# Quantising w1 and w3 to three values: a magnitude compare times half signs, with the signs formed on GpSimd

## The reference

```
xn = layernorm(x)
# recurrent branch (L = 256)
y      = gelu(xn @ w_y + b_y)
xb     = xn @ w_x + b_x
conv   = conv_b + sum_k conv_w[k] * xb shifted        # 4 taps over time
gate_x = sigmoid(conv @ w_ig + b_ig)
gate_a = sigmoid(conv @ w_ag + b_ag)
a      = exp(-8 * gate_a * softplus(a_param))
h[t]   = a[t] * h[t-1] + gate_x * conv * sqrt(1 - a^2)
attn   = (h * y) @ w_out + b_out
# feed-forward branch, hidden size 682, weights quantised on the device
s(w)   = mean(|w|)
q(w)   = clip(round(w / s), -1, 1) * s                # -s, 0 or +s
g      = silu(xn @ q(w1).T) * (xn @ q(w3).T)
ffn    = g @ q(w2).T
out    = x + attn + ffn
```

## Time and profile before

| | us |
|---|---|
| three runs | 77.08, 77.18, 77.36 |
| median | 77.18 |
| the profiled execution, its own time | 77.82 |
| its span in the profile | 76.0 |
| TensorE busy | 70.0 (92%) |
| VectorE busy | 60.8 (80%) |
| ScalarE busy | 49.9 (66%) |
| GpSimd busy | 33.4 (44%) |
| granted TensorE clock | 1.00 of full |

### The profile page before, as it was taken

How to read it: one execution, slowest core, us unless ns; L and a number is a source line. 1 busy time by engine, 2 the same in 40 slices (tenths; PEclk the granted TensorE clock), 3 DMA queues, 4 the chain that set the end, 5 groups by cost and what they waited for, 6 DMA issues and landing times.

```text
span 76.0 us, 1062 instructions
## 1 busy us (share of the span) xinstructions
PE 70.0 (92%) x364; PEld 60.1 (79%) x364; DVE 60.8 (80%) x99; ACT 49.9 (66%) x76; POOL 33.4 (44%) x43
## 2 busy tenths in 40 slices
PE   4999879999999799999999999499999999999960
PEld 4999768877887678888888889388888888899950
DVE  4887599999999999999989999169999999400340
ACT  3663714899999999999989768996357429100000
POOL 6385646336661750052007968940007818910000
DMA  0989999910000000000000000000000000340062
GB/s 13 259 212 338 349 405 367 361 67 9 0 0 0 4 0 0 0 0 0 5 1 0 0 9 0 0 0 0 0 0 0 0 0 0 111 165 9 0 207 69
DMA packets 5095, 5.63 MB, mean 74 GB/s; under 512 B 525, under 2 KB 4578, under 8 KB 5090
## 3 DMA queue, kind: packets, MB, share of 16 engines
q1 hardware_dynamic: 4946, 5.55, 21.8%
q10 hardware_dynamic: 144, 0.01, 0.1%
HBM read 4.51 MB, written 1.05 MB: 73 GB/s over the span
## 4 chain that ended last, share of the span: by engine, by line
PE 37%; ACT 33%; DVE 9%; DMA 7%; issue 5%; POOL 3%; SPq 3%; DVEq 0%; ACTq 0%
PE slot L670 12%; PE slot L703 11%; PE slot L714 9%; DMA x_sb<-x 7%; ACT ta L363 4%; POOL g_lo L256 3%; ACT tx L349 3%; ACT conv_hi L342 3%; ACT xn_y L324 3%; PE slot L653 2%; ACT ta L355 2%; SPq L186 2%; ACT g_hi L300 2%; DVE w_raw L515 2%; DVE stats L437 2%
## 5 line engine op out<-in xcount | busy, mean ns | idle before, releaser
L256 POOL TENSOR_TENSOR g_lo<-w_raw,g_hi 128x512 fp32r<-128x512 f32 x10 | 15.9, 1609 | 16.1 <-ACT g_hi L338 16.1
L670 PE MATMUL slot<-xt_lo,w_q 128*128 128x512 f32 x40 | 15.7, 394 | 0.0
L670 PE MATMUL slot<-xt_hi,w_q 128*128 128x512 f32 x40 | 15.7, 393 | 0.0
L703 PE MATMUL slot<-w_q,g_hi 128*128 128x256 f32 x40 | 10.2, 292 | 1.1 <-POOL g_lo L256 1.1
L703 PE MATMUL slot<-w_q,g_lo 128*128 128x256 f32 x40 | 9.8, 282 | 0.0
L332 ACT ACTIVATE w_raw<-slot,scale 128x512 f32<-128x512 f32 x10 | 6.8, 686 | 4.3 <-PE slot L670 4.3
L493 DVE SCALAR_TENSOR_TENSOR conv<-slot,par,conv 128x511 f32<-128x511 f32 (+2 forms) x12 | 9.0, 748 | 0.4
L703 PEld LDWEIGHTS slot<-w_q,g_hi 128*128 128x128 f32 x40 | 7.6, 191 | 1.6 <-POOL g_lo L256 1.6
L670 PEld LDWEIGHTS slot<-xt_lo,w_q 128*128 128x128 f32 x40 | 7.5, 188 | 1.7
L670 PEld LDWEIGHTS slot<-xt_hi,w_q 128*128 128x128 f32 x40 | 7.5, 188 | 1.7
L338 ACT ACTIVATE g_hi<-w_raw 128x512 fp32r<-128x512 f32 x10 | 6.3, 630 | 3.4 <-DVE w_raw L515 3.2
(11 more groups left out here) (105 smaller groups left out, 143.1 us busy)
## 6 DMA issues: line engine op xcount, KB each, us to landing
w_raw<-w13t SPq DMA_DIRECT2D x2, 682.0 KB, 8.1
w_raw<-dense SPq DMA_DIRECT2D x5, 256.0 KB, 5.7
out<-x_sb SPq DMA_DIRECT2D x3, 256.0 KB, 2.2
w_raw<-w2t SPq DMA_DIRECT2D x1, 640.0 KB
x_sb<-x SPq DMA_DIRECT2D x4, 128.0 KB, 2.2
x_sb<-x SPq DMA_DIRECT2D x1, 512.0 KB, 5.4
out<-x_sb SPq DMA_DIRECT2D x2, 128.0 KB, 1.7
w_raw<-w2t SPq DMA_DIRECT2D x2, 42.0 KB
```

The source lines that it names most:

```text
L256: nc.gpsimd.tensor_tensor(g_lo[:, j, s], g[:, n % RING], g_hi[:, j, s].bitcast(f32), ALU.subtract).then_inc(g_lo_set, 1)
L670: mm = nc.tensor.matmul(slot[H_SLOT[s][j]][:, o], w13_q[:, c, col:col + P], v[:, s, c], start=(c == 0 and v is xt_hi), stop=(c == KC - 1 a ...
L703: mm = nc.tensor.matmul(out_tile(s, i, t), v[:, s, rows], w2_q[:, j], start=(first and j == 0 and t == tiles.start and k == 0), stop=(not ...
```

## The change

The quantisation of w1 and w3 is written as a product. With h(w) = +0.5 where w >= 0 and -0.5 elsewhere, `w13_q = (|w| > s/2) * h(w)`, which is half of the old value; the scale of w1 and w3 is doubled in return.

- |w|: the Abs passes of ScalarE now write to `abs13`, which is kept until it has been read. `abs13` lies in a new tensor `mult_ta` that also holds `mult` and `ta`. Its 22 gap columns are cleared by a GpSimd memset. Because later writers share the memory, ScalarE waits for `w13_q_set` ahead of `gate_a(1)`, and the small memset of `mult` on VectorE moves behind the quantisation.
- h(w): GpSimd forms it in two `tensor_scalar` passes (`half_signs`, 128 x 1408 and 128 x 1364 elements, f32 to bf16) into `below`. They stand between the `lo_of_conv` calls.
- VectorE does one `scalar_tensor_tensor` for each part where it did a `tensor_scalar` and a `scalar_tensor_tensor`, and one threshold less.

```diff
+            def half_signs(cols, loaded):
+                pool.wait_ge(loaded, 16)
+                pool.wait_ge(gaps_set, 1)
+                nc.gpsimd.tensor_scalar(below[:, :, cols], w13_raw[:, :, cols], 0.0, 0.5, ALU.is_ge, ALU.subtract).then_inc(sign_set, 1)
...
-            for s in range(SEQS):
-                for c in range(KC):
-                    lo_of_conv(s, c)
+            lo_of_conv(0, 0)
+            half_signs(slice(0, W3_AT), w1_loaded)
+            lo_of_conv(0, 1)
+            half_signs(slice(W3_AT, W13), w3_loaded)
+            lo_of_conv(1, 0)
+            lo_of_conv(1, 1)
...
-            abs_sum_of(w13_raw[:, :, 0:HIDDEN], KC, junk_a, 0, abs13_set)
+            abs_of(abs13[:, :, 0:HIDDEN], w13_raw[:, :, 0:HIDDEN], 0, abs13_set)
...
             gate_x(1)
+            act.wait_ge(w13_q_set, 2)
             gate_a(1)
...
-                nc.vector.tensor_scalar(thr[:, 1], sums13, -0.5 / WEIGHTS, None, ALU.mult).then_inc(thr_set, 1)
-                nc.vector.tensor_scalar(scale[:, 0:2], sums13, 1.0 / WEIGHTS, None, ALU.mult).then_inc(thr_set, 1)
+                nc.vector.tensor_scalar(scale[:, 0:2], sums13, 2.0 / WEIGHTS, None, ALU.mult).then_inc(thr_set, 1)
...
-                for i, cols in enumerate(parts):
-                    nc.vector.tensor_scalar(below[:, :, cols], w13_raw[:, :, cols], thr[:, 1, i:i + 1], None, ALU.is_lt).then_inc(below_set, 1)
-                for i, cols in enumerate(parts):
-                    dve.wait_ge(below_set, i + 1)
-                    nc.vector.scalar_tensor_tensor(out=w13_q[:, :, cols], in0=w13_raw[:, :, cols], scalar=thr[:, 0, i:i + 1],
-                                                   in1=below[:, :, cols], op0=ALU.is_gt, op1=ALU.subtract).then_inc(w13_q_set, 1)
+                    dve.wait_ge(sign_set, i + 1)
+                    nc.vector.scalar_tensor_tensor(out=w13_q[:, :, cols], in0=abs13[:, :, cols], scalar=thr[:, 0, i:i + 1],
+                                                   in1=below[:, :, cols], op0=ALU.is_gt, op1=ALU.mult).then_inc(w13_q_set, 1)
```

More of the change, by code:

```diff
@@ L73, in build @@
         w2_q = sb("w2_q", [P, FULL + 1, D], f32r)
-        mult = sb("mult", [P, SEQS, KC, SEQ])
+        mult_ta = sb("mult_ta", [P, 2 * SEQS * KC * SEQ])
+        mult = mult_ta[:, 0:SEQS * KC * SEQ].rearrange("p (s c n) -> p s c n", s=SEQS, c=KC)
+        ta = [mult_ta[:, i * KC * SEQ:(i + 1) * KC * SEQ].rearrange("p (c n) -> p c n", c=KC) for i in (3, 2)]
+        abs13 = mult_ta[:, 0:KC * W13].rearrange("p (c n) -> p c n", c=KC)
         conv = sb("conv", [P, SEQS, KC, SEQ])
@@ L78, in build @@
         tx = sb("tx", [P, SEQS, KC, SEQ])
-        ta = sb("ta", [P, SEQS, KC, SEQ])
         g_hi = sb("g_hi", [P, FULL, SEQS, SEQ], f32r)
@@ L101, in build @@
         abs_sum = sb("abs_sum", [P, 4])
-        thr = sb("thr", [P, 2, 2])
+        thr = sb("thr", [P, 1, 2])
         scale = sb("scale", [P, 3])
@@ L217, in _ @@
             nc.gpsimd.memset(w2_raw[:, FULL, :], 0.0).then_inc(gaps_set, 1)
+            nc.gpsimd.memset(abs13[:, :, HIDDEN:W3_AT], 0.0).then_inc(abs_gap_set, 1)
             pool.wait_ge(consts_set, 1)
@@ L299, in abs_sum_of, with abs_of @@
                     out = out.rearrange("p (c n) -> p c n", c=chunks)
-                nc.scalar.activation(out, src, ACT.Abs, accum_out=abs_sum[0:parts, col:col + 1]).then_inc(done, 1)
+                abs_of(out, src, col, done)
+            def abs_of(out, src, col, done):
+                nc.scalar.activation(out, src, ACT.Abs, accum_out=abs_sum[0:src.shape[0], col:col + 1]).then_inc(done, 1)
             act.wait_ge(par_loaded, 16)
@@ L460, in threshold_13, with first_mult @@
                 nc.vector.tensor_scalar(thr[:, 0], sums13, 0.5 / WEIGHTS, None, ALU.mult).then_inc(thr_set, 1)
-                nc.vector.tensor_scalar(thr[:, 1], sums13, -0.5 / WEIGHTS, None, ALU.mult).then_inc(thr_set, 1)
-                nc.vector.tensor_scalar(scale[:, 0:2], sums13, 1.0 / WEIGHTS, None, ALU.mult).then_inc(thr_set, 1)
+                nc.vector.tensor_scalar(scale[:, 0:2], sums13, 2.0 / WEIGHTS, None, ALU.mult).then_inc(thr_set, 1)
             def ternary_13():
-                dve.wait_ge(thr_set, 2)
-                dve.wait_ge(gaps_set, 1)
+                dve.wait_ge(thr_set, 1)
+                dve.wait_ge(abs_gap_set, 1)
+                dve.wait_ge(abs13_set, 2)
                 parts = (slice(0, W3_AT), slice(W3_AT, W13))
                 for i, cols in enumerate(parts):
-                    nc.vector.tensor_scalar(below[:, :, cols], w13_raw[:, :, cols], thr[:, 1, i:i + 1], None, ALU.is_lt).then_inc(below_set, 1)
-                for i, cols in enumerate(parts):
-                    dve.wait_ge(below_set, i + 1)
-                    nc.vector.scalar_tensor_tensor(out=w13_q[:, :, cols], in0=w13_raw[:, :, cols], scalar=thr[:, 0, i:i + 1],
-                                                   in1=below[:, :, cols], op0=ALU.is_gt, op1=ALU.subtract).then_inc(w13_q_set, 1)
+                    dve.wait_ge(sign_set, i + 1)
+                    nc.vector.scalar_tensor_tensor(out=w13_q[:, :, cols], in0=abs13[:, :, cols], scalar=thr[:, 0, i:i + 1],
+                                                   in1=below[:, :, cols], op0=ALU.is_gt, op1=ALU.mult).then_inc(w13_q_set, 1)
+            def first_mult():
+                dve.wait_ge(w13_q_set, 2)
+                nc.vector.memset(mult[:, :, :, 0:1], 0.5).then_inc(mult0_set, 1)
             def threshold_2():
@@ L601, in _ @@
             ternary_13()
+            first_mult()
             gated_input(0)
```

22 lines of the change are left out of this document (10 added, 12 removed).

## The result

| | before | changed |
|---|---|---|
| median | 77.25 us (77.08 to 77.36, 4 runs) | 83.54 us (82.33 to 83.59, 4 runs) |
| ratio | | 1.0735, 95% interval 1.0601 to 1.0869 |
| span of the profiled execution | 76.0 us | 81.7 us |
| mean granted TensorE clock | 1.000 | 0.979 |

The forecast was 78.2 us, from 77.2 to 79.8. The direction was right and the size was not: +6.3 us where +1.0 was forecast.

The account below looks back on a forecast made before the run. TensorE was taken to bound the kernel between 25 and 48 us. VectorE's relief gained 0 and the held tap addition cost 1.0 us, so 77.18 + 1.0 = 78.2 us, range 77.2 to 79.8.

Parts of the forecast that it names:

- What bounds the kernel: Between 25 and 48 us any delay of TensorE, busy 92% of the span, is paid at the end nearly one for one.
- VectorE's relief: VectorE loses two compares, 3.14 us from 25.26 to 28.40; nothing behind them can use it, gain on the path 0.
- the lock: A VectorE pass reading two SBUF tensors and a GpSimd pass exclude each other for a whole instruction; first comer goes first.
- The length of a sign pass: GpSimd's two new passes: 2.3 us for the first and 2.2 for the second, the first bounded by 1.2 and 3.6.
- the sum: Queue walked through with 2.3 us sign passes: TensorE 1.0 us later, 78.2 us; chance 0.45.
- the upper bound of 3.6 us: Longest sign pass allowed, from a two-input GpSimd pass of 1.30 us for 512 columns; would give +3.3, 80.5 us.
- The tiny additions: VectorE's short tap additions with two SBUF inputs, taken as held by GpSimd passes like long ones; otherwise about 77.3 us.
- Step 3, the tap addition: VectorE's addition for chunk (1, 1) waits 1.05 us behind GpSimd's `lo_of_conv(0, 1)`, so TensorE's `gate_product(0, WAG)` starts 1.0 us later.
- The rival of slow signs: GpSimd sign passes of 2.5 to 3.6 us make the last remainder late: +1.3 to +3.3, 78.5 to 80.5 us; chance 0.20.

Follow-up runs that it names:

- with 3.8 us: Changed kernel with the compare alone, no subtraction, in both GpSimd sign passes: 81.42 us, ratio 1.0454.
- easing the addition: Changed kernel with the last conv chunk's three-column addition written as three one-column additions with one SBUF tensor input each: 83.81 us, ratio 1.0717.
- 2.57 us passes: Changed kernel with each sign pass over one of the two feature chunks, the other chunk's signs a constant: 78.19 us, ratio 1.0117.
- the kernel with two waits filled: Changed kernel with ten needless matmuls in TensorE's two late waits for conv_lo of sequence 1 (3 and 7): 83.46 us.

## Why the prediction was wrong

- **What bounds the kernel: right.** TensorE's place between 25 and 48 us was paid one for one, 5.66 us at the first hidden product and 5.7 in the span, and VectorE's relief was worth nothing (77.72 us without sign passes). Of the 3.14 us only 1.7 reached VectorE even there, because the lock took the rest.
- **The length of a sign pass: this is the step that failed.** The term was 2.3 us, bounded by 1.2 and 3.6; it measured 4.98. I took the affine select as the nearest row and a two-input pass of 512 columns as the upper bound, on the unspoken ground that a pass with one input cannot cost more a column than one with two. It does: 3.4 ns a column against 2.5. The bounds were drawn from other operations, and the rows of a large `tensor_scalar` on GpSimd were missing. With it the path changed: the sum had TensorE wait for the last tap, and it waited 5.18 us for the remainders behind the sign passes. The steps themselves carry the longer pass (80.0 to 81.5 expected, 81.42 measured, with 3.8 us). With the upper bound of 3.6 us the sum would have been 80.5, and the range stopped at 79.8 even so. The estimates of 2.1 and 1.2 us that stood beside it, from the Trainium skill (GPSIMD Engine Reference, sections Elementwise — side-by-side cycle accounting and Engine selection), were further off for this form, though the multiply-add and the copy, 1.36 us each, are close to its line rate.
- **The lock: right.** The tiny additions are caught, the first slips in and the second does not, and quantising passes and remainders take turns. Wrong was "for a whole instruction": a compare-subtract pass of 4.98 us frees the lock 1.0 us before its recorded end, and one of 2.49 us at least 1.3 us before. The Trainium skill (SBUF — State Buffer, Who interferes with whom) also has the engine that issues first hold the shared pair for the whole instruction; for GpSimd's two-input passes the trace agrees within 0.15 us, for this one the measurement decides.
- **Step 3, the tap addition, +1.0 on TensorE: right in kind, without effect here.** It was held, but with 4.98 us the remainder ahead of it was later still, and easing the addition changed nothing (83.81 us). It was the only cost in the sum, and no run shows it being paid: with 2.57 us passes, the nearest to the forecast's 2.3, the addition came 0.2 us ahead of the remainder that was to hold it, and the stretch grew by 0.2 us. Whether a pass of 2.3 us would bring the 1.0 is not shown. That 78.19 us was measured at 2.57 is luck as far as the steps go.
- **The rival of slow signs** named the right mechanism, with +3.3 at its far end. Its upper pass length, 3.6 us, was still short, and it had no term for the clock, which adds 1.3 to 1.45 us where it falls behind the last wait. The trace of before shows 1.00 throughout, and I did not ask what waits of 2 us would do to it.

## What to carry to other kernels

An operation that the trace does not show is not bounded by other operations that seem heavier; measure it by itself first, or let the range say that it can be twice as long. Ahead of moving work to GpSimd, list what it shares with VectorE and what stands behind it in its queue; idle time between short passes (here under 2 us at a time) does not hold a pass of 5. And a busy engine is not a bound: VectorE was busy 24 of 25 us, and 1.7 us less on it, all that came of 3 us less work, were worth nothing.

## What was not expected of the hardware

- GpSimd's `tensor_scalar` on 1408 columns of f32 takes 4.97 us for compare-subtract, 3.77 for a compare or a multiply alone, and 1.36 for multiply-add, the same as a copy. Two steps can be cheaper than one.
- GpSimd's compare-subtract pass of 4.98 us lets VectorE's two-input instructions go 1.0 us before its recorded end, one of 2.49 us at least 1.3 us before, the compare alone (3.65 us) about 0.8, a two-input subtraction 0.15.
- Behind TensorE's waits of 0.80 and 1.81 us the granted clock was 0.50 until 37.7, some 3 us in all; behind one of 2.42 us, in the kernel with two waits filled, it was 0.50 for over 6 us; in another execution of the changed kernel it stayed at 1.00 for 1.7 us of matmuls behind a wait of 2.45 us and was then 0.50 for 3.4 us.
